# Region ends first, fills from two queues, and tile tables made across partitions, in a graph-convolution and expert kernel

## The reference

```
edge_index = jnp.stack([src, dst])
x = x + gnn(_layernorm(x), edge_index, ...)
x = x + ffn(_layernorm(x)[None], ...)[0]

def ffn(features, ...):
    rh = relu(features @ router_w1 + router_b1)
    expert_logits = softmax(rh @ router_w2 + router_b2)
    top_w, top_i = top_k(expert_logits, 2)
    routing_weights = softmax(top_w)
    h1 = relu(einsum('bsd,edh->bseh', features, expert_w1) + expert_b1)
    h2 = relu(einsum('bseh,ehf->bsef', h1, expert_w2) + expert_b2)
    expert_out = einsum('bsef,efo->bseo', h2, expert_w3) + expert_b3
    sel = take_along_axis(expert_out, top_i[..., None], axis=2)
    return sum(sel * routing_weights[..., None], axis=2)
```

## Time and profile before

| what | us |
|---|---|
| median of three runs | 5498.24 (5498.19 to 5498.49) |
| the profiled execution, its own time | 5502.19 |
| the profiled execution, span from first to last instruction | 5500.4 |
| TensorE busy | 4465.1 (81%) |
| POOL busy | 3389.7 (62%) |
| VectorE busy | 1839.7 (33%) |
| ACT busy | 1203.7 (22%) |

### The profile page before, as it was taken

The page is one execution under the profiler, slowest core; times in us unless marked ns, Lnnn a source line. Parts: engine busy times, 40 slices in busy tenths (PEclk is TensorE's granted clock), DMA queues, the critical chain, the costliest instruction groups (busy, mean ns, idle before and its releaser), DMA issues. The chain is left out here.

```text
span 5500.4 us, 79307 instructions
## 1 busy us (share of the span) xinstructions
PE 4465.1 (81%) x15178; PEld 2034.9 (37%) x15179; DVE 1839.7 (33%) x6850; ACT 1203.7 (22%) x2776; POOL 3389.7 (62%) x3633
## 2 busy tenths in 40 slices
PE   5578888888888888777888888878888866499999
PEld 4322222222222222222222222222222234388888
DVE  7422222222222222332222222222222247666665
ACT  6201111111111101230111111111111137455554
POOL 0377777777777777557777777777777734311111
PEclk5677666766777766777666676677666667799999
DMA  4743333333333333353333333333333333411111
GB/s 115 220 134 105 105 105 105 105 105 105 105 105 105 105 105 105 94 148 105 105 105 105 105 105 105 105 105 105 105 105 105 105 85 101 133 50 48 49 49 45
DMA packets 261867, 564.55 MB, mean 103 GB/s; under 512 B 67263, under 2 KB 136225, under 8 KB 261794
## 3 DMA queue, kind: packets, MB, share of 16 engines
q0 software_dynamic: 171264, 466.46, 29.0%
q1 hardware_dynamic: 90530, 97.27, 6.2%
HBM read 503.39 MB, written 60.09 MB: 102 GB/s over the span
## 5 line engine op out<-in xcount | busy, mean ns | idle before, releaser
L638 POOL DMA_INDIRECT ring<-messages,idx_stage x3328 | 3149.5, 946 | 1180.4 <-issue 750.0
L1669 PE MATMUL ps<-ring,onehot_mem 128*64 128x256 f32 x6656 | 2910.0, 545 | 737.1 <-DMA ring<-messages,idx_stage 677.0
L1669 PEld LDWEIGHTS ps<-ring,onehot_mem 128*64 128x64 f32 x6656 | 849.0, 174 | 2437.9 <-DMA ring<-messages,idx_stage 2132.4
L1143 DVE TENSOR_TENSOR acc<-acc,ps 128x128 f32 x832 | 239.8, 288 | 3128.0 <-PE ps L1567 3126.7
L766 ACT ACTIVATE win_rows<-ps 64x256 f32<-64x256 f32 x832 | 313.7, 377 | 1862.8 <-PE ps L1669 1848.2
L1132 DVE TENSOR_SCALAR onehot_mem<-iota_bf,tables 128x64 f32<-128x64 bf16 x3344 | 632.7, 271 | 101.3 <-issue 53.8
L691 POOL DMA_INDIRECT out_dram<-acc x128 | 128.7, 1005 | 597.4 <-DVE acc L1520 416.4
L755 ACT ACTIVATE idx_stage<-tables 128x8 int32 (+1 forms) x420 | 87.4, 209 | 1868.4 <-PE ps L1669 1867.8
L1872 PE MATMUL ps<-acc 128*128 128x256 f32 x2048 | 465.8, 380 | 0.8 <-ACT acc L945 0.8
L1872 PEld LDWEIGHTS ps<-acc 128*128 128x128 f32 x2048 | 384.1, 190 | 53.7 <-issue 1.2
L1567 PEld LDWEIGHTS ps<-ident,win_rows 64*128 64x128 f32 x1664 | 207.9, 175 | 494.6 <-issue 494.6
(11 more groups left out here) (256 smaller groups left out, 2003.6 us busy)
## 6 DMA issues: line engine op xcount, KB each, us to landing
ring<-messages,idx_stage POOLq DMA_INDIRECT x3328, 2.8
rows_mem<-in_x_dram SPq DMA_DIRECT2D x54, 448.0 KB, 4.2
acc<-routed_rows SPq DMA_DIRECT2D x64, 264.0 KB, 3.0
messages<-dinvT SPq DMA_DIRECT2D x23, 448.0 KB, 5.5
dinvT<-in_x_dram SPq DMA_DIRECT2D x22, 448.0 KB, 4.2
messages<-ring SPq DMA_DIRECT2D x19, 448.0 KB, 4.0
dinvT<-dinv_row SPq DMA_DIRECT2D x28, 224.0 KB, 3.4
messages<-rows_mem SPq DMA_DIRECT2D x14, 448.0 KB, 3.8
```

Source lines behind the costliest of these rows:

```text
L638: pool.indirect_dma_start(out=slots[:, s, :], out_offset=None, in_=t_dram[layer], in_offset=bass.IndirectOffsetOnAxis(ap=idx_stage[:, u, s ...
L1143: dve.tensor_tensor(sums(w, WIN), sums(w, WIN), ps[:, 2 + u, 0:KH * WIN].rearrange("p (k w) -> p k w", k=KH), ALU.add).then_inc(ev_fast, 1)
L1669: pe.matmul(ps[0:WIN, u, 0:D], onehot[:, u, j, 0:WIN], slots[:, s, :], start=j == 0, stop=j == CPG - 1).then_inc(chunks_used, 1)
```

## The change

It makes the same regions, fills and tiles in another way:
- `tail_int` is one addition from PSUM, the first thing after `counted`, and `tiles_known` is 1 with it. The six small memsets of `wx` move from ahead of `fill` to behind the table.
- The spare fill waits for `fill_ready` alone. The other fifteen are split: SP makes regions 7 to 14 and ACT regions 0 to 6, and each loads its end and issues its fill before it goes to the next (`fill_region`).
- The number of tiles of a region comes by adding 255 and shifting right by 8. The running sums come by one product with a triangle (`up_to`) and one reduction. All is computed on 128 partitions; partition t stands for tile t, so comparing the sums with the partition's number (`part_no`) gives the regions behind tile t as 15 elements. One product over 3 x 15 elements and one reduction give the three entries of a tile (two expert numbers and the address).
- Three TensorE transposes make these columns three rows of 128 in PSUM, and VectorE copies them to `tile_int` on partition 0, from which SP and ACT load as before.
- POOL makes the triangle and the new constants with the other masks; VectorE makes `part_no` and one of the bases beside them.

```diff
+        def fill_region(eng, e):
+
+            tail = eng.value_load(tail_int[0:1, e:e + 1], min_val=e * XR, max_val=e * XR + NPAD)
+            eng.dma_start(routed[bass.ds(tail, TOK), :].rearrange(whole, b=TB), fill_flat).then_inc(filled, 16)
...
+            sp.wait_ge(fill_ready, 1)
+            sp.dma_start(routed[NDUO * XR:NDUO * XR + TOK, :].rearrange(whole, b=TB), fill_flat).then_inc(filled, 16)
             sp.wait_ge(tiles_known, 1)
-            tails = [sp.value_load(tail_int[0:1, e:e + 1], min_val=e * XR, max_val=e * XR + NPAD) for e in range(NDUO)]
-            sp.wait_ge(fill_ready, 1)
-            whole = "(p b) f -> p (b f)"
-            fill_flat = fill.rearrange("p b f -> p (b f)")
-            sp.dma_start(routed[NDUO * XR:NDUO * XR + TOK, :].rearrange(whole, b=TB), fill_flat).then_inc(filled, 16)
-            for tail in tails:
-                sp.dma_start(routed[bass.ds(tail, TOK), :].rearrange(whole, b=TB), fill_flat).then_inc(filled, 16)
+            for e in range(NDUO // 2, NDUO):
+                fill_region(sp, e)
...
+            pool.memset(up_to, 1.0).then_inc(masks_made, 1)
+            pool.wait_ge(masks_made, 3)
             pool.affine_select(out=tri_f, in_=tri_f, compare_op=ALU.is_gt, fill=0.0, base=0, pattern=[[1, RB]],
                                channel_multiplier=-1).then_inc(masks_made, 1)
+            pool.affine_select(out=up_to, in_=up_to, compare_op=ALU.is_ge, fill=0.0, base=0, pattern=[[1, NDUO], [-1, NDUO]],
+                               channel_multiplier=0).then_inc(masks_made, 1)
             for e in range(NX):
                 pool.memset(mark[:, e:e + 1], -float(1 << (NX - 1 - e)))
             for n, (a, b) in enumerate(DUOS):
                 pool.memset(duo_mark[:, n:n + 1], -float((1 << (NX - 1 - a)) + (1 << (NX - 1 - b))))
             for n, duo_next in enumerate(DUOS[1:] + DUOS[-1:]):
-                pool.memset(first_step[:, n:n + 1], float(duo_next[0] - DUOS[n][0]))
-                last = pool.memset(second_step[:, n:n + 1], float(duo_next[1] - DUOS[n][1]))
+                pool.memset(steps_of[:, 0, n:n + 1], float(duo_next[0] - DUOS[n][0]))
+                pool.memset(steps_of[:, 1, n:n + 1], float(duo_next[1] - DUOS[n][1]))
+            for n, (base, limit) in enumerate(((0.0, BIG), (1.0, BIG), (0.0, float(NDUO * XR)))):
+                pool.memset(tile_base[:, n:n + 1], base)
+                last = pool.memset(tile_limit[:, n:n + 1], limit)
             last.then_inc(masks_made, 1)
...
+            act.wait_ge(fill_ready, 1)
+            act.wait_ge(tiles_known, 1)
+            for e in range(NDUO // 2):
+                fill_region(act, e)
             act.wait_ge(experts_in, 16 * NEXPERT)
             act.wait_ge(tiles_known, 2)
...
-            dve.wait_ge(masks_made, 4)
+            dve.wait_ge(masks_made, 6)
             dve.tensor_copy(tri_bf, tri_f)
             step(dve.tensor_copy(node_ids, iota_pb[0:RB, :]))
+            step(dve.tensor_copy(part_no, iota_pb[:, 0:1]))
+            dve.tensor_scalar(tile_base[:, 2:3], part_no, float(TOK), None, ALU.mult)
...
             dve.wait_ge(zb_done, NCH)
-            for e in range(NX):
-                dve.memset(wx[:, e, EA - 1:EA], -float(1 << (NX - 1 - e)))
             step(dve.memset(fill, 0.0))
             step(dve.tensor_scalar(fill[:, :, D:D + 1], iota_pb[:, 0:1].unsqueeze(1).to_broadcast([P, TB, 1]),
                                    float(NPAD), None, ALU.add))
             dve.memset(marker[:, 0, 4:5], 0.0).then_inc(fill_ready, 1)
             dve.wait_ge(counted, 1)
-            dve.tensor_copy(count, ps[0:1, 7, 0:NDUO])
...
-            for e in range(1, NDUO):
-                step(dve.tensor_tensor(last_tile[:, e:e + 1], last_tile[:, e - 1:e], last_tile[:, e:e + 1], ALU.add))
...
-            for n, steps_of in enumerate((first_step, second_step)):
-                step(dve.tensor_tensor(jump, behind, steps_of.unsqueeze(1).to_broadcast([1, TILES, NDUO]), ALU.mult))
-                step(dve.tensor_reduce(tile_e[:, n, :], jump, AX.X, ALU.add))
...
+            dve.tensor_tensor(tail_int, ps[0:1, 7, 0:NDUO], region_start[0:1, :], ALU.add).then_inc(tiles_known, 1)
+            step(dve.tensor_scalar(n_int, ps[:, 7, 0:NDUO], float(TOK - 1), None, ALU.add))
+            step(dve.tensor_scalar(n_int, n_int, TOK.bit_length() - 1, None, ALU.arith_shift_right))
+            step(dve.tensor_copy(n_tiles, n_int))
+            dve.tensor_scalar(steps_of[:, 2, :], n_tiles, -float(TOK), float(XR), ALU.mult, ALU.add)
+            step(dve.tensor_tensor(up_to_now, up_to, n_tiles.unsqueeze(1).to_broadcast([P, NDUO, NDUO]), ALU.mult))
+            step(dve.tensor_reduce(last_tile, up_to_now, AX.X, ALU.add))
+            step(dve.tensor_scalar(behind, last_tile, part_no, None, ALU.is_le))
+            step(dve.tensor_tensor(jump, steps_of, behind.unsqueeze(1).to_broadcast([P, 3, NDUO]), ALU.mult))
+            step(dve.tensor_reduce(tile_of, jump, AX.X, ALU.add))
+            step(dve.tensor_tensor(tile_of, tile_of, tile_base, ALU.add))
+            dve.tensor_tensor(tile_of, tile_of, tile_limit, ALU.min).then_inc(tile_of_ready, 1)
+            for e in range(NX):
+                dve.memset(wx[:, e, EA - 1:EA], -float(1 << (NX - 1 - e)))
+            dve.wait_ge(tile_of_turned, 1)
+            dve.tensor_copy(tile_int, ps[0:1, 6, 0:3 * P].rearrange("p (j t) -> p j t", j=3)).then_inc(tiles_known, 1)
...
+            pe.wait_ge(tile_of_ready, 1)
+            for j in range(3):
+                last = turn(ps[0:1, 6, j * P:(j + 1) * P], tile_of[:, j:j + 1])
+            last.then_inc(tile_of_turned, 1)
```

More of the change, by code:

```diff
@@ L260, in gnn_moe @@
         mark, duo_mark, region_start = old_dinv.take(RB, NX), old_dinv.take(RB, NDUO), old_dinv.take(RB, NDUO)
-        first_step, second_step = old_dinv.take(1, NDUO), old_dinv.take(1, NDUO)
+        steps_of = old_dinv.take(P, 3, NDUO)
+        up_to = old_dinv.take(P, NDUO, NDUO)
+        part_no, tile_base, tile_limit = old_dinv.take(P, 1), old_dinv.take(P, 3), old_dinv.take(P, 3)
         tri_bf = old_dinv.take(RB, RB // 2).bitcast(BF16)
@@ L273, in gnn_moe @@
         run_add = old_dinv.take(RB, NDUO)
-        old_rows = Region(dinvT[:, 0:4 * BPC * D])
-        reached = old_rows.take(1, NDUO, LEVELS)
-        behind, jump = old_rows.take(1, TILES, NDUO), old_rows.take(1, TILES, NDUO)
         old_ring, old_tables = Region(ring), Region(tables)
@@ L297, in gnn_moe @@
         wterm, wsel = old_acc.take(P, 2, 2, TB), old_acc.take(P, 2, 2, TB)
[L298 to L303, removed]
+        n_int, n_tiles, last_tile, behind = [old_acc.take(P, NDUO) for _ in range(4)]
+        n_int = n_int.bitcast(I32)
+        up_to_now, jump = old_acc.take(P, NDUO, NDUO), old_acc.take(P, 3, NDUO)
+        tile_of = old_acc.take(P, 3)
+        tail_int, tile_int = old_acc.take(1, NDUO).bitcast(I32), old_acc.take(1, 3, P).bitcast(I32)
         RANKS = 128
@@ L353, in gnn_moe @@
         masks_made, ones_made, counted, fill_ready, filled = sem("masks_made"), sem("ones_made"), sem("counted"), sem("fill_ready"), sem("filled")
-        tiles_known, rows_in = sem("tiles_known"), sems("rows_in", 2)
+        tiles_known, tile_of_ready, tile_of_turned, rows_in = sem("tiles_known"), sem("tile_of_ready"), sem("tile_of_turned"), sems("rows_in", 2)
         xh_ready, tile_turned, xT_done, expert_a, expert_b = sem("xh_ready"), sem("tile_turned"), sem("xT_done"), sem("expert_a"), sem("expert_b")
@@ L444, in half @@
             return (t - u) // 2 if isinstance(t, int) else t // 2
+        whole = "(p b) f -> p (b f)"
+        fill_flat = fill.rearrange("p b f -> p (b f)")
+        def fill_region(eng, e):
+            tail = eng.value_load(tail_int[0:1, e:e + 1], min_val=e * XR, max_val=e * XR + NPAD)
+            eng.dma_start(routed[bass.ds(tail, TOK), :].rearrange(whole, b=TB), fill_flat).then_inc(filled, 16)
         def routing(eng, body):
@@ L920, in expert_of @@
             def expert_of(s, x):
[L921 removed]
+                return act.value_load(tile_int[0:1, x, bass.ds(s, 1)], min_val=0, max_val=NX - 1)
             def take_hidden(s, u, x, e):
@@ L1464, in _ @@
-            step(dve.tensor_copy(last_tile, n_tiles))
-            for e in range(1, NDUO):
-                step(dve.tensor_tensor(last_tile[:, e:e + 1], last_tile[:, e - 1:e], last_tile[:, e:e + 1], ALU.add))
-            dve.tensor_tensor(count, count, region_start[0:1, :], ALU.add)
-            dve.tensor_scalar(skip, n_tiles, -float(TOK), float(XR), ALU.mult, ALU.add)
-            step(dve.tensor_tensor(behind, tile_no.unsqueeze(2).to_broadcast([1, TILES, NDUO]),
-                                   last_tile.unsqueeze(1).to_broadcast([1, TILES, NDUO]), ALU.is_ge))
@@ L1471, in _ @@
-            dve.tensor_copy(tail_int, count).then_inc(tiles_known, 1)
-            for n, steps_of in enumerate((first_step, second_step)):
```

(10 more changed lines are left out.)

12 lines of the change are left out of this document (2 added, 10 removed).

## The result

The kernel after takes 5488.3 us (median of 15 runs, 5485.5 to 5490.3), the kernel before beside it 5499.9. The ratio is 0.9979, with a 95% interval of 0.9972 to 0.9986: 11.6 us faster, and by the interval between 7.7 and 15.4. The ratio lies just beyond the bound of 0.2%, but the interval reaches to both sides of it, so whether the gain is larger than 0.2% stays open. 12.8 us were forecast.

The account below looks back on a forecast made before the run. TensorE's idle gap of 34.5 us between routing and expert tiles was taken as the bound. First fill 15.68 us earlier, less 2.9 for scatters, gives 12.8 off: 5498.24 becomes 5485.4 us; 8-in-10 range 5482.2 to 5489.4.

Parts of the forecast that it names:

- the table: VectorE's tile-number work at the seam: ready at about 4767, ten us before SP or ACT asks, so costing nothing.
- The fill phase: Sixteen region fills before the first tile: still bound by their bytes on two queues, 12.2 us at 355 GB/s.
- the collision: POOL's last eight scatters share the DMA engines with the fills: 2.9 us added, bounded by nothing and twice 2.9.
- A region at 1.15 us a queue: Register load about 0.605 plus fill issue 0.55 on SP or ACT; two queues offer a fill each 0.58 us.
- The clock: TensorE's lower clock (0.5) at the first tile: 2.8 us long, losing 1.4, taken as unchanged; bounds -1.4 and +1.4.
- the three signs of being wrong: At the seam: gap ends on a late ACT instruction, DMA share clearly below 0.9, or lower clock through more of first tile.
- More comes off: Rival at the seam: scatters cost nothing or two queues feed more bytes; 16.5 us off, 5481.7; chance 0.14.
- The dearer collision: Rival at the fills: scatters cost twice as much, 9.9 us off, or 8.5 with longer lower clock; joint chance 0.20.
- the slower rival: Rival on ACT's queue: fills issued there are dear; at 6 us a region the kernel takes 5514; chance 0.04.
- the scatters hold the first tile as long as before: Rival at the seam: SP waits for the scatters instead, so the change does nothing, 5498.2; chance 0.04.

Follow-up runs that it names:

- old-table run: The kernel after with tile numbers still worked out on partition 0 by the old products and reductions; ratio to the kernel before 0.9979.
- loads-first run: The kernel after, but SP and ACT each load all their region ends, then issue all their fills; ratio to the kernel before 0.9982.
- more-fills run: The kernel after with four more fills of unread regions on ACT, behind its own seven, which SP also awaits; ratio to the kernel before 0.9990.
- one-queue run: The kernel after with all fifteen regions on SP and none on ACT; ratio to the kernel before 0.9985.
- apart run: The kernel after, but SP and ACT wait for all scatters ahead of their first fill; ratio to the kernel before 0.9992.

## Why the prediction was right, and by how much it was off

**The place and the mechanism: right.** The gain is the seam's, and it comes from the first fill's start: 15.57 us earlier measured from C, 15.68 forecast. The ends (first operation behind `counted`), the spare fill ahead of the ends, and the loads behind the transfers all stand in the timeline as written. The old-table run shows that the table was rightly costed at nothing. In all the seam became 10.3 us shorter in the profiled pair (9.6 and 10.8 by the other two traces), where 12.8 were forecast.

**The fill phase: right kind, wrong size.** The forecast said that the fills of two queues stay bound by their bytes, and the share of 0.96 to 1.01, the loads-first run and the more-fills run bear it out but for the last microsecond. The term of the sum that was mis-sized is the collision: +2.9 us forecast, +4.97 measured (19.31 - 14.34; +4.7 to +5.7 over three traces). I had bounded it by 0 and 5.8 us, and the value lies inside. The queues' shares split it. The scatters' busy time was 3.07 us before (19.1% of 16.1 us) and is 3.63 beside the fills (18.7% of 19.4 us), and the fills' own rose from 11.96 to 12.16: together 3.83 us more for the engines in this phase. The other 1.1 us are engines that stand idle at its start and at its end, where one or two of them, or SP's last fill, come later than the rest. So the step took the scatters' cost as their busy time alone (2.9 for 3.1). It missed that the two kinds together cost 0.8 us more than apart, and that a phase lasts until its last engine is done (1.1 us), which a sum of bytes over the mean rate leaves out.

**A region at 1.15 us a queue: wrong with two queues, nearly right with one.** With the engines behind, a load took 1.0 us, and a region 1.9; in the one-queue run it was 1.21. The DMA engines were full meanwhile, so of the slower region only the last fill's lateness can have cost time: 0.6 us by the apart run.

**The clock: just outside its bounds in the profiled pair, and chance.** There the first tile ran at 0.5 for 6.1 us (4780.95 to about 4787.05) instead of 2.8, which costs 1.6 us more. I had taken no change and bounded it by 1.4. This is the one of the three signs of being wrong that showed. It is not the change's doing as far as the traces tell: the stretch lasted 3.2 and 3.8 us in the other two traces of the kernel after, and 3.2 to 5.6 in those of its variants without products. That of before is the shortest of all. Over all traces without products the tile stage took 703.5 to 705.3 us, and before had the 703.5. So one trace of before flatters it.

**The number: near, and partly by luck.** The seam and the clock together give 8.6 us in the profiled pair (8.6 to 10.3 over three traces of after), below the 11.6 of the medians but within the interval of 7.7 to 15.4. That the medians come within 1.2 us of the 12.8 is better than the parts deserve: the collision alone missed by 2.1.

**The rest of the 14.2 us between the two spans** is most likely not the change: C itself stands 5.6 us earlier in the trace of after. Over the six traces of spans near 5500 us, with nearly the same code ahead of C, it lies anywhere from 4754.7 to 4767.4.

**The rivals.** "More comes off" is out: two queues don't raise the rate. The dearer collision happened in part (2.1 us more than forecast). ACT's fills are as cheap as SP's (0.34 and 0.33 us), so the slower rival is out. That the scatters hold the first tile as long as before is out too: it comes 10.3 us earlier.

**The chances.** 0.72 on faster by over 0.2% was somewhat bold: with the mis-sized collision the gain (0.21%) came to stand on that bound.

## What to carry to other kernels

When work is moved from a serial stretch into a shared one, first ask which resource each piece is bound by: here the loads and the order could be hidden, the bytes could not, and the bytes that already lived in the new place came on top. Put the cheap, early thing (the start of the transfers) first; a rewrite of arithmetic beside it was elegant and worth nothing that these runs can tell, because the old arithmetic, 14 us long, was covered by the fills already. And size a transfer phase by its last engine, not by the mean rate: here idle engines at the start and the end were 1.1 us of the 5.0 by which it grew. Last, take more than one trace of a kernel before reading a difference of 1 us: three of the same kernel lay that far apart.

## What the runs showed of the hardware

- A register load on SP took 0.27 us in the median with no fill in flight (kernel before), 0.32 between fills while the DMA engines had idle time (one queue, share 0.72 near the end), and 1.02 between fills while they were full (kernel after, share 0.96 to 1.01; ACT 0.95). In the loads-first run the fills' issues took 1.25 us instead. In these runs the wait showed on whichever instruction stood behind a fill in the queue.
- Fills in pieces of 2112 bytes beside scatters in rows of 1056 bytes moved 308 GB/s at a share of 0.96, and fills alone 355 GB/s at 0.98. The scatters' busy time was 3.63 us beside the fills and 3.07 without.
- One DMA engine of sixteen can run on by itself for up to 2.5 us (share 0.06), and SP, which waits for all of them, goes on only behind it.
- TensorE's granted clock was 0.5 in the first tile after pauses of 1.30, 2.85 and 2.94 us between the filler products and the turns, and stayed at 1.0 where no pause stood there. That the pause is the cause is not shown; the runs differ in the length of the work ahead of it too.
- The kernel before took 5500 to 5507 us on some chips and 6255 to 6307 on others. The kernel after's time from C to the end was 731.5 us on the former and 730.8 and 729.9 on the latter, so the difference lies ahead of C.
